# Per-bank row tiles for the logits of a two-layer graph attention kernel, with one ScalarE row operand from two transposes

## The reference

```python
h = jnp.einsum('bnd,ade->bane', feat_in, W)
th = jnp.tanh(h)
attn_src = jnp.einsum('bane,aeo->bano', th, w_src)
attn_dst = jnp.einsum('bane,aeo->bano', th, w_dst)
attn = attn_src + jnp.swapaxes(attn_dst, 2, 3)
attn = jnp.where(attn >= 0, attn, LEAKY_ALPHA * attn)
...
attn = jax.nn.softmax(attn, axis=-1)
feat_out = jnp.einsum('banm,bame->bane', attn, h) + b
```

## Time and profile before

| | us |
|---|---|
| median of 3 runs | 1130.89 (1130.64 to 1131.96) |
| the profiled execution | 1132.1 |
| its span, first to last instruction | 1130.2 |
| TensorE busy | 1073.2 (95%) |
| ScalarE busy | 919.4 (81%) |
| VectorE busy | 897.2 (79%) |
| GpSimd busy | 765.2 (68%) |

### The profile page before, as it was taken

One profiled execution on the slowest core, in us unless ns is written; L12 is line 12 of the kernel. 1 busy time (PEld: TensorE's weight loads), 2 busy tenths in 40 slices (PEclk: granted clock), 3 DMA queues, 4 the chain that ended last, 5 costly groups with the idle time before them and its releaser, 6 DMA issues.

```text
span 1130.2 us, 25501 instructions
## 1 busy us (share of the span) xinstructions
PE 1073.2 (95%) x8236; PEld 883.3 (78%) x8236; DVE 897.2 (79%) x1828; ACT 919.4 (81%) x3383; POOL 765.2 (68%) x909
## 2 busy tenths in 40 slices
PE   6889999999999999999999999999999999997774
PEld 5678888888888888878888888888888888786652
DVE  5457878888887888888788888878888887888874
ACT  3348888888888888888888888888888888888874
POOL 1367776676777667677766767776676777667652
PEclk9999999999999999999999999999999999999986
DMA  9101010020101002010100201010020101000000
GB/s 270 56 2 57 15 68 18 8 71 16 64 15 61 26 8 71 16 64 15 62 26 8 71 15 64 15 60 27 8 72 16 64 15 43 16 8 16 16 15 21
DMA packets 25893, 44.66 MB, mean 40 GB/s; under 512 B 2462, under 2 KB 23714, under 8 KB 25762
## 3 DMA queue, kind: packets, MB, share of 16 engines
q1 hardware_dynamic: 23234, 41.91, 10.9%
q10 hardware_dynamic: 2496, 1.12, 0.5%
q0 software_dynamic: 32, 0.00, 0.0%
HBM read 30.43 MB, written 12.58 MB: 38 GB/s over the span
## 4 chain that ended last, share of the span: by engine, by line
PE 57%; POOL 23%; issue 9%; DVE 6%; ACT 3%; DMA 2%; POOLq 0%; ACTq 0%; DVEq 0%
PE ps_b L253 13%; PE ps_d L253 13%; POOL z L964 9%; PE ps_a L253 7%; PE ps_d L459 5%; POOL xT_lo L916 4%; PE ps_a L382 3%; PE ps_s L362 3%; PE ps_s L354 3%; PE ps_d L447 3%; POOL p L991 3%; PE ps_c L469 2%; POOL s L956 2%; POOL thw L999 2%; POOL y L958 2%
## 5 line engine op out<-in xcount | busy, mean ns | idle before, releaser
L583 ACT ACTIVATE z<-z,s 128x128 f32<-128x128 f32 x768 | 297.1, 391 | 1.5 <-DVE s L798 0.9
L964 POOL TENSOR_TENSOR z<-z,mask 128x512 f32<-128x512 f32 x192 | 218.2, 1164 | 0.5 <-ACT z L679 0.5
L583 ACT ACTIVATION_READ_ACCUMULATOR z<-z,s 128x1 f32 x768 | 146.6, 191 | 0.0
L610 ACT ACTIVATE p<-ps_s,s 128x128 f32<-128x128 f32 x384 | 134.7, 378 | 13.1 <-DVE s L776 13.0
L991 POOL TENSOR_TENSOR p<-p,s 128x768 f32<-128x768 f32 x64 | 94.2, 1471 | 61.4 <-DVE s L804 61.4
L459 PE MATMUL ps_d<-ident,z 128*128 128x128 f32 x768 | 118.7, 278 | 9.2 <-ACT z L583 8.2
L953 POOL TENSOR_SCALAR s<-s 128x1 f32<-128x1 f32 x128 | 28.8, 225 | 143.3 <-DVE s L895 131.6
L999 POOL TENSOR_TENSOR thw<-th,w_sd 128x768 f32<-128x768 f32 x64 | 117.4, 1834 | 3.7 <-ACT th L633 3.7
L459 PEld LDWEIGHTS ps_d<-ident,z 128*128 128x128 f32 x768 | 90.6, 143 | 17.6 <-ACT z L583 9.1
L679 ACT ACTIVATE z<-ps_d 128x512 f32<-128x512 f32 x192 | 100.8, 598 | 1.2 <-PE ps_d L447 1.2
L945 POOL TENSOR_TENSOR xb<-xb,bf_all 128x768 f32<-128x768 f32 x32 | 58.6, 1834 | 58.6 <-DVE sd L878 55.5
(11 more groups left out here) (154 smaller groups left out, 3448.5 us busy)
## 6 DMA issues: line engine op xcount, KB each, us to landing
x_cols<-in_xT_dram SPq DMA_DIRECT2D x16, 768.0 KB, 6.4
xb<-in_x_dram SPq DMA_DIRECT2D x16, 768.0 KB, 4.9
out_dram<-y SPq DMA_DIRECT2D x64, 192.0 KB, 1.8
z<-in_L_gnn_Wq_dram SPq DMA_DIRECT2D x1, 576.0 KB, 6.4
p1T<-in_L_gnn_Wk_dram SPq DMA_DIRECT2D x1, 576.0 KB, 8.7
qT<-in_L_gnn_Wv_dram SPq DMA_DIRECT2D x1, 576.0 KB, 11.1
kT<-in_L_gnn_Wf_dram SPq DMA_DIRECT2D x1, 576.0 KB, 13.4
z<-in_L_gnn_W_dram SPq DMA_DIRECT2D x1, 576.0 KB, 11.7
```

What stands on the lines that cost most here:

```text
L583: done = act.activation(z[:, a, :], z[:, a, :], ACT.Exp, bias=neg1[:, a:a + 1], accum_out=sum1[:, a:a + 1])
L610: last = act.activation(p0[:, o, i, :], ps_s[:, o, i * N:(i + 1) * N], ACT.Exp, bias=neg0[:, k:k + 1], accum_out=sum0[:, k:k + 1])
L964: pool.tensor_tensor(z[:, 4 * q:4 * q + 4, :], z[:, 4 * q:4 * q + 4, :], mask[:, t, :].unsqueeze(1).broadcast_to([P, 4, N]), ALU.add).then ...
```

## The change

Each of the three logits matmuls now has 32 partitions of its own for operands: bank q uses partitions 32q to 32q + 31 of `rows_L` and `cols_R`, of which 24 rows carry something (three terms of four source scores against ones, and ones against three terms of four target scores). For that the 16-bit terms are stored in six groups of 32 columns (`sd_parts`, 128 x 192) instead of two of 64. Two transposes read overlapping windows of it, columns 0 to 95 and 84 to 179, and write 96 partitions of bank `ps_c` and of bank `ps_a`; the ones stand in `sd_parts` from the start (two small GpSimd memsets). ScalarE makes `rows_L` with one copy, VectorE `cols_R` with one product over 96 partitions. The two fills on VectorE are gone.

```diff
-        rows_L = sb("rows_L", [P, 3, N], BF16)
+        rows_L = sb("rows_L", [P, N], BF16)
...
+        sd_parts = sb("sd_parts", [P, 6 * 32], BF16)
+        part = [sd_parts[:].rearrange("p (s c) -> p s c", c=32)[:, :, 4 * t:4 * t + 4] for t in range(3)]
+        sd_rows, sd_cols = sd_parts[:, 0:96], sd_parts[:, 84:180]
+        ps_rows, ps_cols = (bank[0:96, D:D + N // 2].bitcast(BF16) for bank in (ps_c, ps_a))
...
-                pe.transpose(ps_t, sd3_wide[:].rearrange("p s w -> p (s w)"), ident_b[:]).then_inc(S["sd_turned"], 1)
+                pe.transpose(ps_rows, sd_rows, ident_b[:]).then_inc(S["sd_turned"], 1)
+                pe.transpose(ps_cols, sd_cols, ident_b[:]).then_inc(S["sd_turned"], 1)
...
+                pe.wait_ge(S["rows_ready"], t + 1)
                 pe.wait_ge(S["cols_ready"], t + 1)
                 for q in range(3):
-                    pe.wait_ge(S["rows_ready"], 3 * t + q + 1)
+                    tile = slice(32 * q, 32 * (q + 1))
...
-                    last = pe.matmul(heads, rows_L[:, q, :], cols_R[:], start=True, stop=True)
+                    last = pe.matmul(heads, rows_L[tile, :], cols_R[tile, :, :], start=True, stop=True)
...
-                        for q in range(3):
-                            act.activation(rows_L[0:64, q, :], ps_t[0:64, :], ACT.Copy, scale=of_bank[0:64, q:q + 1]
-                                           ).then_inc(S["rows_ready"], 1)
+                        act.activation(rows_L[0:96, :], ps_rows, ACT.Copy).then_inc(S["rows_ready"], 1)
...
-                dve.wait_ge(S["padding_ready"], 2)
-                dve.tensor_copy(rows_L[64:P, :, :], of_bank[64:P, :].unsqueeze(2).broadcast_to([64, 3, N])
-                                ).then_inc(S["pick_ready"], 1)
-                dve.tensor_copy(cols_R[0:64, :, :], of_slot[0:64, :].unsqueeze(2).broadcast_to([64, 4, N])
-                                ).then_inc(S["pick_ready"], 1)
...
-                        dve.wait_ge(S["sd_turned"], tl + 1)
+                        dve.wait_ge(S["sd_turned"], 2 * (tl + 1))
...
+                        dve.tensor_tensor(cols_R[0:96, :, :], ps_cols.unsqueeze(1).broadcast_to([96, 4, N]),
+                                          of_slot[0:96, :].unsqueeze(2).broadcast_to([96, 4, N]), ALU.mult
                                           ).then_inc(S["cols_ready"], 1)
...
+            pool.memset(sd_rows.rearrange("p (q c) -> p q c", c=32)[:, :, 12:24], 1.0).then_inc(S["sd_padded"], 1)
...
+            pool.memset(sd_cols.rearrange("p (q c) -> p q c", c=32)[:, :, 0:12], 1.0).then_inc(S["sd_padded"], 1)
```

More of the change, by code:

```diff
@@ L112, in build_program @@
         thw = sb("thw", [P, 2, D])
[L113 to L117, removed]
+        sd = sb("sd", [P, 6, 4])
+        sd_rest = sb("sd_rest", [P, 2, 6, 4])
+        sd_parts = sb("sd_parts", [P, 6 * 32], BF16)
+        part = [sd_parts[:].rearrange("p (s c) -> p s c", c=32)[:, :, 4 * t:4 * t + 4] for t in range(3)]
+        sd_rows, sd_cols = sd_parts[:, 0:96], sd_parts[:, 84:180]
+        ps_rows, ps_cols = (bank[0:96, D:D + N // 2].bitcast(BF16) for bank in (ps_c, ps_a))
         z = sb("z", [P, H1, N])
@@ L865, in iteration @@
                         dve.wait_ge(S["sd_ready"], tl + 1)
-                        if due(tl):
-                            dve.wait_ge(S["sd_turned"], tl)
-                        dve.tensor_copy(sd3[:, :, 0, :], sd[:]).then_inc(S["split_small"], 1)
+                        if tl == 0:
+                            dve.wait_ge(S["sd_padded"], 3)
+                        else:
+                            dve.wait_ge(S["sd_turned"], 2 * tl)
+                        dve.tensor_copy(part[0], sd[:]).then_inc(S["split_small"], 1)
                         dve.wait_ge(S["split_small"], 4 * tl + 1)
-                        dve.tensor_tensor(sd_rest[:, 0, :, :], sd[:], sd3[:, :, 0, :], ALU.subtract
+                        dve.tensor_tensor(sd_rest[:, 0], sd[:], part[0], ALU.subtract
                                           ).then_inc(S["split_small"], 1)
                         dve.wait_ge(S["split_small"], 4 * tl + 2)
-                        dve.tensor_copy(sd3[:, :, 1, :], sd_rest[:, 0, :, :]).then_inc(S["split_small"], 1)
+                        dve.tensor_copy(part[1], sd_rest[:, 0]).then_inc(S["split_small"], 1)
                         dve.wait_ge(S["split_small"], 4 * tl + 3)
-                        dve.tensor_tensor(sd_rest[:, 1, :, :], sd_rest[:, 0, :, :], sd3[:, :, 1, :], ALU.subtract
+                        dve.tensor_tensor(sd_rest[:, 1], sd_rest[:, 0], part[1], ALU.subtract
                                           ).then_inc(S["split_small"], 1)
                         dve.wait_ge(S["split_small"], 4 * tl + 4)
-                        dve.tensor_copy(sd3[:, :, 2, :], sd_rest[:, 1, :, :]).then_inc(S["sd3_ready"], 1)
+                        dve.tensor_copy(part[2], sd_rest[:, 1]).then_inc(S["sd3_ready"], 1)
                     if tail:
@@ L920, in _ @@
             pool.memset(ones_b[:], 1.0)
-            pool.memset(sd3_wide[:], 0.0).then_inc(S["padding_ready"], 1)
+            pool.memset(sd_parts[:], 0.0).then_inc(S["sd_padded"], 1)
+            pool.wait_ge(S["sd_padded"], 1)
+            pool.memset(sd_rows.rearrange("p (q c) -> p q c", c=32)[:, :, 12:24], 1.0).then_inc(S["sd_padded"], 1)
+            pool.wait_ge(S["sd_padded"], 2)
+            pool.memset(sd_cols.rearrange("p (q c) -> p q c", c=32)[:, :, 0:12], 1.0).then_inc(S["sd_padded"], 1)
             pool.memset(hb_rows[:], 0.0).then_inc(S["padding_ready"], 1)
@@ L934, in moved_constants @@
                 pool.wait_ge(S["hb_small"], 5)
-                pool.wait_ge(S["padding_ready"], 2)
+                pool.wait_ge(S["padding_ready"], 1)
                 pool.dma_start(hb_rows[0:3, :], hb_split[:]).then_inc(S["hb_moved"], 16)
@@ L1042 @@
     held["ident"] = _np.eye(P, dtype=_np.float32)
-    head = _np.arange(3 * H1) % H1
-    half = _np.zeros((P // 2, 7), _np.float32)
-    half[_np.arange(3 * H1), head // 4] = 1.0
-    half[_np.arange(3 * H1), 3 + head % 4] = 1.0
-    held["pick"] = _np.concatenate([half, half])
+    row = _np.arange(P)
+    held["pick"] = ((row % 32 < 24)[:, None] & (row[:, None] % 4 == _np.arange(4)) & (row < 96)[:, None]
+                    ).astype(_np.float32)
     arrays, args = {}, []
```

14 lines of the change are left out of this document (5 added, 9 removed).

## The result

| | us |
|---|---|
| median after, 4 runs | 1118.38 (1115.61 to 1121.06) |
| median before, 4 runs beside them | 1130.78 (1130.64 to 1131.96) |
| ratio | 0.9882, 95% interval 0.9867 to 0.9898 |
| profiled execution after | 1119.08, span 1117.3 |

The change is faster by 1.2% by the ratio on record (the two medians alone give 0.9890). Direction and mechanism held, the size did not.

A forecast was written before the change was run, and what follows sets the result against it. TensorE was taken to bound the kernel, except from the V step's `sd3` to the next line 362, where GpSimd does. Loop 7.6, start 1.6, end 0: 9.2 off 1132.1, less 1.2, gives 1121.7 us, range 1117.5 to 1127.5.

The forecast's parts named there:

- Second transpose: On TensorE before the logits: a second transpose costs 0.07 and moves `cols_R` and the first logits matmul by 0.07.
- One row operand: On ScalarE: two of three copies go, so the next `p1T` copy ends at 669.16 instead of 669.41.
- The failed step: Third logits matmul behind `p1T`: lag near today's 0.15 rather than the quick 0.05, so 0.18 gained a step.
- Row tiles run together: Logits matmuls on 32 rows each: three start almost together once open, the third's gate alone setting the end.
- rival 1: Logits matmuls: the tiles take turns, line 344 0.04 later, loop loses 1.7 against 1.6, total 1131 us; chance 0.08.
- Leaving the tiles: Line 344 behind the third logits matmul: the tile-shape change drains, so it starts 0.38 - 0.07 after the third.
- Rival 2: Line 344 behind the logits: no drain on leaving and the quick wait, 0.35 gained a step, total 1114.6 us; chance 0.07.
- The V step's gain lost at line 362: First softmax transposes after the V step: GpSimd sets the pace, so only three of four steps' gains count.
- The margins of `fT` and GpSimd: Before lines 477 and 362: `fT` has room for 0.35, GpSimd's product some 0.40, both larger than the gain.
- rival 3: Freed steps: another engine takes over, gain held to 0.05 to 0.11, total 1124.5 to 1127.5 us; chance 0.10.
- Start: Before the loop: without VectorE's two fills line 344 starts 1.3 sooner, perhaps 0.7 more by the clock; 1.6 taken.
- End: Last steps without projections: +0.3 through `cols_R`, some 0.3 perhaps given back by ScalarE; net 0.

The follow-up runs named there:

- e1: The changed kernel measured again as it is, to learn its spread: 1118.56 us, ratio 0.9876 to the kernel before.
- e2: The changed kernel with the row operand made in three ScalarE copies again, each logits matmul waiting for its own: 1139.05 us, ratio 1.0069.
- e9: The changed kernel with each logits matmul again waiting for two semaphores, row operand and its bank's p1T evacuation: 1126.8 us, ratio 0.9948.
- e4: The changed kernel with all three logits matmuls on rows 0 to 31, one and the same row tile: 1131.4 us, ratio 0.9992.
- e7: The changed kernel with the next element's mask product (line 344) ahead of the logits: 1125.56 us, ratio 0.9933.
- e3: The kernel before with one ScalarE copy of the row operand used for all three banks, matmuls on all 128 rows: 1125.0 us, ratio 0.9932.
- e5: The changed kernel with all three logits matmuls on rows 0 to 95 instead of row tiles: 1126.0 us, ratio 0.9937.
- e10: The changed kernel with turn_x1 (line 409) ahead of turn_f, the logits still ahead of the mask product: 1123.37 us, ratio 0.9919.
- e13: The changed kernel with turn_x1 ahead of turn_f only in the steps that have projections: 1122.84 us, ratio 0.9907.
- e14: The changed kernel with the mask product ahead of the logits everywhere, turn_x1 ahead of turn_f only in steps with projections: 1109.65 us, ratio 0.9804.

## Why the prediction was wrong

The span of the profiled run against that of before, 1130.2 to 1117.3, cut at the starts of line 409:

| stretch | predicted | measured |
|---|---|---|
| start, to the first line 409 | -1.6 | +0.1 (-0.9 in e1) |
| first four steps and 13 groups | -7.6 | -11.6 |
| last eight steps and what follows | 0 | -1.4 |
| sum | -9.2 | -12.9 |

- *Second transpose*: right (0.05 and its shift of 0.08). First logits matmul at T + 1.25 against 1.28 (from a step 0.04 later than the median of before, 1.17).
- *One row operand*: `p1T` ends at T + 1.35, where I had 669.16 - 667.80 = 1.36. Right.
- *The failed step*: the lag of the third matmul. I had both rows, 0.15 with two waits and 0.05 with one, named the quick one, and took 0.18 "near today's lag, since it is the same wait behind the same copy". It measured 0.05, so the term of 0.18 a step was 0.26. The cause is the number of waits: the same tiles with two waits follow `p1T` by 0.145 (e2), and one wait put back costs each matmul 0.10 to 0.13 (e9). The matmul's form had changed and the nearest row was the one with its number of waits. Taken so, the gain is 0.26, 42 x 0.26 = 10.9, and 12.5 with the start: 1118.4. That this meets the measured median is luck, since the start gave less than its 1.6 and the end more than its 0.
- *Row tiles run together*: right (0.006 apart), but only with rows of their own, and so close only with one wait (0.126 with two), which the prediction did not say. e4, where they are made to take turns, is rival 1: no gain.
- *Leaving the tiles*: right, line 344 0.32 behind the third against my 0.31. Rival 2 fell with it: its quick wait came, its missing price did not.
- *The V step's gain lost at line 362*: right, in every kernel here the median of the step behind it is 16.24 to 16.29, whatever the logits take.
- *The margins of `fT` and GpSimd*: right for this change (line 478 waits 3.1 us in 4 waits, where line 477 had 2.5 in 4), rival 3 fell. e7 shows the room: 0.26 later is too late.
- *Start*: too high by cover I did not see. The fill's 1.76 was mostly VectorE beside GpSimd's `xT_lo`, and without it a later cast stood there instead; line 344's idle time fell by 0.88 (2.04 to 1.16), not by 1.3, and it came 0.67 sooner. The granted clock stayed full at 38 to 40 as hoped, but in the profiled run it was at half from 59.5 on, and nothing of the gain was left.
- *End*: set at 0, gave 2.0 behind the last line 409 (35.9 to 33.9). e3, with one copy and no tiles, has 34.0 there, e2, with tiles and three copies, 35.7, which points to ScalarE's copies. It is not shown: e5 (34.9), e10 (35.2) and e4 (36.3) have one copy too, and the granted clock there differs from kernel to kernel (0.64 to 0.80). The seven steps ahead lost 0.55 in the profiled run and won 0.8 in e1.

Open stays what decides where the clock falls; runs of one kernel lie up to 6 us apart, the longer ones at a lower mean clock (e13). The miss of 3.7 in the span is 4.0 in the loop, of which the lag is 42 x 0.08 = 3.4, 1.4 at the end, less 1.7 at the start.

## What to carry to other kernels

Count the waits of an instruction, not only its work: on TensorE one more wait, even one long met, cost 0.10 to 0.13 us where nothing hid it, and putting one back on each logits matmul took over half of this change (ratio 0.9948 against 0.9882 and, in e1, 0.9876). Test a packed matmul together with what feeds it, since the tiles alone lost 0.16 a step and with ScalarE's part won 0.26. Before crediting a deletion with its duration, look at what the other engine on the same memory ran in that time.

## What the hardware showed unexpectedly

- Matmuls on row tiles of their own, writing banks of their own, run together: the first two start 6 ns apart, and in e14, where no gate holds them, all three start 3 ns apart and last 0.39 together. On the same 32 rows they are 0.215 apart, as on all 128.
- A wait met long before delays its matmul: 0.126 between tiles with two waits, 0.006 with one.
- Kernels with steps equal to 0.03 us differ by 5 us in the median (e1 1118.6, e10 1123.4). Of the 6.0 between their profiled spans 3.8 lie in the last seven steps and 1.2 at the start, where e10's granted clock was lower, and 1.3 behind the last line 409.
